# An AdaLN block with WKV attention and a mixture of experts: engine queues reordered from the third step on

## The chip, the cores and the metric

The kernel runs on one core of a Trainium2 chip. The metric is the device time of one execution in microseconds (us); the time of a kernel is the median of its runs. A difference of about 0.3% between two kernels can be told from none.

The engines are named as the profile names them: PE is TensorE (matmuls and transpositions), PEld its weight loads, DVE is VectorE, ACT is ScalarE, POOL is GpSimd, SP is SyncE, which here only issues transfers. Each engine works through its own queue of instructions in the order in which the program issues them, and waits where an instruction needs a semaphore.

## The reference

The input `x` is 4 x 1024 x 256 in float32. What is computed, cut to what matters:

```
mod = silu(c) @ wmod                          # six shift, scale and gate vectors per batch
h = layernorm(x) * (1 + ca) + sa
xk, xv, xr = mixes of h and h shifted by one token
k, v, r = xk @ Wk.T, xv @ Wv.T, xr @ Wr.T
wkv = the WKV scan over the 1024 tokens       # running maximum, running sums aa and bb
x = x + ga * ((sigmoid(r) * wkv) @ Wo.T)
h = layernorm(x) * (1 + cb) + sb
logits = h @ gate_w.T; top 2 of 8 experts, softmax over the two
y = sum over e of comb[e] * ((silu(h @ Wg[e]) * (h @ Wu[e])) @ Wd[e])
    + (silu(h @ sWg) * (h @ sWu)) @ sWd       # a shared expert of twice the width
x = x + gb * y
```

## The kernel before

**Tiling.** The 4096 tokens are cut into eight chunks of 512 (`NC` = 8, two per batch row). Most tiles hold the 256 features as two halves of 128 partitions with 512 tokens each; an operation on one half is 128x512, on both 128x1024. The eight experts of width 64 are taken in four pairs, and the shared expert makes a fifth block (`NB` = 5).

**Steps.** The work is pipelined over chunks. `step(n)` exists once for each engine and issues that engine's part for up to four chunks: the input norm, mixes and projections of chunk n + 1 (`nxt`), the end of attention and the second norm of chunk n (`cur`), the experts of chunk n - 1 (`prev`), and the last residual of chunk n - 2 (`before`). DVE also takes the input statistics of chunk n + 2 (`after`). The program runs a start for chunk 0, then step 0 (on ACT and DVE a `first_step` of its own), and steps 1 to 9. The order within a step is written out by hand in each engine's function, and this order with the semaphores decides when everything runs.

**Who does what in a step.**
- PE: `turn1` transposes the normalised input; `up(prev, i)`, i = 0 to 9, computes the experts' two products, six matmul groups on high and low parts each; `logits`, `turn_logits`, `turn_comb` and `spread_comb` belong to the routing; `attn` is the output projection of attention, `project(nxt, j)`, j = 0 to 5, are k, v and r in two halves each; `turn_attn` and `turn_down` transpose results back; `down(prev, 0)` and `down(prev, 1)` are the experts' second product; `turn2` transposes the second norm.
- ACT: `normalise1` and `normalise2` (4 instructions each), `affine1`, `affine2` (writes `h2_h` and `h2`), `part_mix`, `add_bias`, `tanh_r`, `silu`, the exponentials, `reciprocal_seed`, `attn_out`, `down_out`, and loads of function tables.
- DVE: `stats1`, `stats2`, `mix`, `scan_max`, `scan_sums`, `out_sums` 0 to 4, `divide` 0 to 3, `route` (19 small steps), `gate_up` (a product), `weigh`, `residual1`, `residual2`, and `low_part`, which subtracts `h2_h` from `h2` and releases `up(prev, 0)`.
- POOL: `rstd`, four small operations per norm and chunk, between the statistics on DVE and the normalisation on ACT.
- SP: loads of input chunks into two buffers `x_in`, stores of output chunks. A load into a buffer waits until `residual1` has read the chunk before it in that buffer.

The eight PSUM banks are shared: `mm` 0 to 3 by projections and `up`, `yo` 0 and 1 by `attn`, `turn_attn`, `down` and `turn_down`, `tp` and `cb` by the transpositions of norms and the routing. A wait ahead of each group on PE names whose reading frees its bank. The names in the profile's rows are those of the tiles: `n_xn` is a normalised chunk, `h_h` and `h_l` are `h2_h` and `h2_l`, `pool_x` holds `h2`, the weights `wmod` and two of the three `x1` buffers, `pool_n` holds `num` and `den`, `pool_g` the gates.

## Time and profile before

| | us |
|---|---|
| median of 3 runs | 409.92 |
| lowest, highest | 408.98, 410.11 |
| profiled execution, whole | 408.2 |
| its span | 406.3 |
| PE busy in the span | 366.6 |
| DVE busy | 334.6 |
| ACT busy | 295.2 |
| POOL busy | 44.7 |

The span is the time from the first to the last instruction that the profile shows; the whole time of the same execution is 1.9 us more. Busy times overlap, since engines work side by side. A timeline row gives the start, the time until the group's last end, and in brackets how long the engine was idle before and whose work ended that. Matmuls are pipelined, so the starts of two groups tell more than the length of one.

### The profile page before, as it was taken

The numbers are of one execution on the slowest core, as the hardware profiler recorded it, in microseconds if no ns is written. First come the engines' busy times: TensorE is split into PE (matmuls) and PEld (weight loads), VectorE is DVE, ScalarE is ACT, GpSimd is POOL, SyncE is SP. The second block draws the span as 40 slices with busy tenths as digits, with TensorE's granted clock in tenths as the row PEclk, the third lists the DMA queues.
The fourth block names the chain that finished last, engine by engine and source line by source line (L and its number), as shares of the span: only waits on it lengthen the run. The fifth ranks groups of instructions, "written<-read, shape, count | busy, mean of one in ns | idle before, by whom it ended". The sixth has DMA issues, their size and how long they took to land.

```text
span 406.3 us, 4276 instructions
## 1 busy us (share of the span) xinstructions
PE 366.6 (90%) x1348; PEld 224.8 (55%) x1348; DVE 334.6 (82%) x667; ACT 295.2 (73%) x466; POOL 44.7 (11%) x76
## 2 busy tenths in 40 slices
PE   4892873999999999999999999999999999969985
PEld 4561332756565845675476646574567455725752
DVE  4799989987989898999899898989898988541541
ACT  2699699846997589948994799759985894324332
POOL 4030013001400050002200230005000200010000
PEclk9995795799999999999999999999999999969999
DMA  8900010001000110011000300011001000100011
GB/s 287 268 5 1 0 52 0 0 2 52 0 2 0 52 52 2 0 52 54 0 2 2 103 0 0 2 53 50 2 1 52 2 0 0 52 2 0 0 53 52
DMA packets 15626, 13.27 MB, mean 33 GB/s; under 512 B 4690, under 2 KB 15092, under 8 KB 15604
## 3 DMA queue, kind: packets, MB, share of 16 engines
q1 hardware_dynamic: 15572, 12.99, 10.4%
q8 instruction: 11, 0.18, 0.2%
q14 instruction: 11, 0.09, 0.1%
q10 hardware_dynamic: 32, 0.01, 0.0%
HBM read 8.80 MB, written 4.19 MB: 32 GB/s over the span
## 4 chain that ended last, share of the span: by engine, by line
PE 63%; ACT 22%; DVE 9%; issue 3%; DMA 1%; SPq 0%; DVEq 0%; ACTq 0%
PE mm L737 29%; PE mm L632 10%; PE yo L765 7%; PE yo L650 7%; ACT arg L391 6%; ACT n_xn L326 5%; PE yo L659 3%; ACT arg L417 3%; ACT pool_x L366 2%; ACT h_h L365 2%; ACT kv L374 2%; DVE h_l L979 2%; ACT arg L405 1%; PE cb L749 1%; DVE mixed L879 1%
## 5 line engine op out<-in xcount | busy, mean ns | idle before, releaser
L632 PE MATMUL mm<-mixed,WT 128*128 128x512 f32 x192 | 87.5, 604 | 8.1 <-DVE mixed L879 8.1
L765 PE MATMUL yo<-act,w_dn 128*128 128x512 f32 x160 | 74.1, 613 | 5.4 <-DVE act L1056 5.4
L632 PEld LDWEIGHTS mm<-mixed,WT 128*128 128x128 f32 x192 | 36.3, 193 | 53.4 <-issue 39.6
L737 PE MATMUL mm<-h_h,w_up_h 128*128 128x512 f32 x160 | 55.2, 426 | 4.3 <-DVE h_l L979 4.3
L765 PEld LDWEIGHTS yo<-act,w_dn 128*128 128x128 f32 x160 | 30.8, 197 | 41.9 <-issue 35.6
L737 PE MATMUL mm<-h_l,w_up_h 128*128 128x512 f32 x160 | 51.1, 401 | 0.0
L737 PE MATMUL mm<-h_h,w_up_l 128*128 128x512 f32 x160 | 51.0, 400 | 0.0
L300 POOL TENSOR_TENSOR n_ve<-n_mv,small 128x4 f32<-128x4 f32 x16 | 8.2, 510 | 310.9 <-DVE n_mv L868 310.9
L374 ACT ACTIVATE kv<-mm,cols 128x512 f32<-128x512 f32 x32 | 21.8, 682 | 18.9 <-PE mm L632 18.9
L737 PEld LDWEIGHTS mm<-h_h,w_up_h 128*128 128x128 f32 x160 | 28.4, 192 | 12.6 <-DVE h_l L979 6.4
L737 PEld LDWEIGHTS mm<-h_h,w_up_l 128*128 128x128 f32 x160 | 30.6, 191 | 7.5
L737 PEld LDWEIGHTS mm<-h_l,w_up_h 128*128 128x128 f32 x160 | 30.6, 191 | 7.5
L879 DVE SCALAR_TENSOR_TENSOR mixed<-hT,cols,mixed 128x512 f32<-128x512 f32 x48 | 33.5, 742 | 0.3 <-ACT mixed L385 0.2
L438 ACT ACTIVATE pool_g<-mm 128x512 f32<-128x512 f32 x40 | 23.4, 586 | 10.4 <-PE mm L737 10.4
L385 ACT ACTIVATE mixed<-hT,rest 128x512 f32<-128x512 f32 x48 | 30.9, 710 | 0.0
L650 PE MATMUL yo<-pool_n,WT 128*128 128x512 f32 x64 | 28.8, 592 | 0.0
L1056 DVE TENSOR_TENSOR act<-cb,pool_g 128x512 f32<-128x512 f32 x24 | 16.5, 687 | 13.1 <-PE cb L749 13.1
L303 POOL TENSOR_TENSOR n_rstd<-n_ve,small 128x4 f32<-128x4 f32 x16 | 24.4, 1526 | 1.3
L1049 DVE TENSOR_TENSOR pool_g<-mm,pool_g 128x512 f32<-128x512 f32 x32 | 21.1, 680 | 3.7 <-PE mm L737 3.7
L979 DVE TENSOR_TENSOR h_l<-pool_x,h_h 128x1024 fp32r<-128x1024 f32 x8 | 9.8, 1225 | 17.3 <-ACT pool_x L366 17.3
L584 PE MATMUL tp<-ident,n_xn 128*128 128x128 f32 x88 | 15.2, 301 | 9.7 <-ACT n_xn L326 6.4
L468 ACT ACTIVATE combT<-cb 16x512 fp32r<-16x512 f32 x8 | 4.7, 588 | 26.2 <-PE cb L698 26.2
(149 smaller groups left out, 662.6 us busy)
## 6 DMA issues: line engine op xcount, KB each, us to landing
x_in<-in_L_attn_x_dram SPq DMA_DIRECT2D x8, 512.0 KB, 3.5
out_dram<-pool_x SPq DMA_DIRECT2D x5, 512.0 KB, 2.9
pool_x<-in_L_wmod_dram SPq DMA_DIRECT2D x2, 512.0 KB, 4.9
out_dram<-x_third SPq DMA_DIRECT2D x2, 512.0 KB, 2.9
pool_x<-in_L_wmod_dram SPq DMA_DIRECT2D x2, 256.0 KB, 4.0
pool_g<-in_L_ffn_Wg_dram SPq DMA_DIRECT2D x2, 256.0 KB, 5.0
pool_g<-in_L_ffn_Wu_dram SPq DMA_DIRECT2D x2, 256.0 KB, 4.4
w_dn<-in_L_ffn_Wd_dram SPq DMA_DIRECT2D x1, 512.0 KB, 3.9
```

Source lines behind the costliest of these rows:

```text
L303: nc.gpsimd.tensor_tensor(norm.rstd[:, :], norm.ve[:, :], small[:, 1, :], ALU.pow).then_inc(norm.pool_step, 1)
L326: nc.scalar.activation(norm.xn[:, t, :], src[:, t, :], ACT.Identity, bias=norm.shift[:, t:t + 1], scale=norm.rstd[:, t:t + 1]).then_inc(no ...
L374: nc.scalar.activation(kv[:, w, kc, :], mm[PROJECT_BANK[j]][:, :], ACT.Identity, bias=bias_cols[w][:, kc:kc + 1]).then_inc(kv_done, 1)
L385: nc.scalar.activation(mixed[:, w, kc, :], hT[c.half][:, kc, 0:CH], ACT.Identity, scale=rest[:, KH * w + kc:KH * w + kc + 1]).then_inc(par ...
L391: nc.scalar.activation(arg[:, j, h, :], tmp[:, h, :], ACT.Relu, scale=sign, bias=bias[:, h:h + 1]).then_inc(relu_done, 1)
L438: nc.scalar.activation(sg[:, e, :], mm[UP_BANK[2 * e]][:, :], ACT.Silu).then_inc(silu_done, 1)
L632: last = nc.tensor.matmul(mm[PROJECT_BANK[j]][:, :], WT[:, w, kc, oc * P:(oc + 1) * P], mixed[:, w, kc, :], start=(kc == 0), stop=(kc == K ...
L650: last = nc.tensor.matmul(yo[oc][:, :], WT[:, O, kc, oc * P:(oc + 1) * P], rw[:, kc, :], start=(kc == 0), stop=(kc == KH - 1))
L737: last = nc.tensor.matmul(mm[UP_BANK[i]][:, :], w[:, kc, gu, e * P:(e + 1) * P], rhs[:, kc, :], start=(n == 0), stop=(n == 3 * KH - 1))
L765: last = nc.tensor.matmul(yo[oc][:, :], w_dn[:, e, oc * P:(oc + 1) * P], act[:, e, :], start=(e == 0), stop=(e == NB - 1))
L879: nc.vector.scalar_tensor_tensor(out=mixed[:, w, kc, :], in0=hT[c.half][:, kc, 1:CH + 1], scalar=mix_cols[w][:, kc:kc + 1], in1=mixed[:, w ...
L1049: nc.vector.tensor_tensor(dst[:, e, :], mm[UP_BANK[2 * e + 1]][:, :], sg[:, e, :], ALU.mult).then_inc(prod_done, 1)
```

## The change

- **Queues.** What was `step` for all chunks is split into `first_step` (step 0), `second_step` (step 1) and `step` (from step 2, the third, on), each with its own order on PE, ACT and DVE.
- **Halves.** `attn`, `turn_attn`, `turn_down`, `turn2` and `tanh_r` are issued by half, each half with the semaphore count of its own half.
- **Routing.** `route` runs in four pieces on DVE, with products and mixes between them.
- **Statistics and sums.** In `step`, `stats2` and `stats1` stand together behind the last `weigh`, ahead of `scan_sums`; `out_sums` 2 and 4 and `low_part` go to the beginning of the following step; in `first_step` `scan_sums(nxt, 0)` stands between `stats2` and `stats1`.
- **First norm of chunk 0.** POOL computes only `rstd`; DVE subtracts the mean and multiplies in one instruction. K's transposition on PE stands behind those of the norm.
- **Output weights.** The copy of Wo, with its factor -0.5, goes from DVE to ACT.
- **Input buffers.** `x_in` has three buffers; a load waits for the chunk three before it.

```diff
-        x_in = [sb(f"x_in{h}", [P, TT, H]) for h in range(2)]
+        x_in = [sb(f"x_in{h}", [P, TT, H]) for h in range(3)]
...
-                wait(sp, x1_done, 2 * (c.n - 1))
-                sp.dma_start(x_in[c.half][:, :, :], x_chunks[c.n]).then_inc(x_loaded[c.half], 16)
+                wait(sp, x1_done, 2 * (c.n - 2))
+                sp.dma_start(x_in[c.n % 3][:, :, :], x_chunks[c.n]).then_inc(x_loaded[c.n % 3], 16)
...
+                direct = norm is norm1 and c.n == 0
...
+                if direct:
+                    return
...
+            ac.wait_ge(w_turned, O + 1)
+            nc.scalar.activation(WT[:, O, :, :], yo[1][:, :].rearrange("p (k h) -> p k h", k=KH), ACT.Identity,
+                                 scale=-0.5).then_inc(wo_done, 1)
...
             def turn2(c, kc):
                 pe.wait_ge(norm2.xn_done, TT * (c.n + 1))
                 if c.n:
-                    pe.wait_ge(act_done, NP * c.n)
+                    pe.wait_ge(act_done, NP * c.n - kc)
...
+            def attn(c, oc):
+                if oc == 0:
+                    pe.wait_ge(rw_done, c.n + 1)
...
                 elif c.n == 1:
-                    pe.wait_ge(x1_done, 2)
+                    pe.wait_ge(x1_done, oc + 1)
                 else:
-                    pe.wait_ge(yT_done, KH * (c.n - 1))
+                    pe.wait_ge(yT_done, KH * (c.n - 2) + oc + 1)
...
+            def turn_attn(c, k):
                 pe.wait_ge(oT_done, KH * (c.n + 1))
                 if c.n >= 2:
-                    pe.wait_ge(x2_done, 2 * (c.n - 1))
-                turn_out(oT, attn_turned)
+                    pe.wait_ge(x2_done, 2 * (c.n - 2) + k + 1)
+                turn_out(oT, k, attn_turned)
...
+            def turn_down(c, k):
                 pe.wait_ge(yT_done, KH * (c.n + 1))
                 if chunk(c.n + 2):
-                    pe.wait_ge(oT_done, KH * (c.n + 3))
-                turn_out(yT, down_turned)
+                    pe.wait_ge(oT_done, KH * (c.n + 2) + k + 1)
+                turn_out(yT, k, down_turned)
...
             def first_step():
...
                 stats2(cur)
+                scan_sums(nxt, 0)
                 stats1(after)
-                scan_sums(nxt, 0)
                 scan_sums(nxt, 1)
...
-            turn_square(K, mm[2])
             pe.wait_ge(norm1.xn_done, TT)
             turn(norm1, chunk(0), 0, tp)
             turn(norm1, chunk(0), 1, cb)
+            turn_square(K, mm[2])
```

The new `step`, from the third step on, on PE, on ACT and on DVE:

```
turn1(nxt, 0); up(prev, 0); logits(prev); turn1(nxt, 1); up(prev, 1); up(prev, 2); turn_logits(prev)
up(prev, 3); up(prev, 4); attn(cur, 0); project(nxt, (0,)); attn(cur, 1); project(nxt, (1,))
turn_down(before, 0); up(prev, 5); turn_down(before, 1); turn_comb(prev); turn_attn(cur, 0)
up(prev, 6); spread_comb(prev, 1); up(prev, 7); spread_comb(prev, 2); up(prev, 8); up(prev, 9)
spread_comb(prev, 3); spread_comb(prev, 4); turn_attn(cur, 1); project(nxt, (2, 3, 4))
down(prev, 0); turn2(cur, 0); turn2(cur, 1); project(nxt, (5,)); down(prev, 1)
```

```
affine2(prev, 0); affine2(prev, 1); normalise1(nxt); reciprocal_seed(cur); affine1(nxt, 0); SILU table
tanh_r(cur, 0); affine1(nxt, 1); logits_out(prev); tanh_r(cur, 1); silu(prev, 0); down_out(before, 0)
part_mix(nxt, 0); part_mix(nxt, 1); silu(prev, 1); part_mix(nxt, 2); down_out(before, 1)
add_bias(nxt, 0); gap_out(prev); attn_out(cur, 0); silu(prev, 2); attn_out(cur, 1); add_bias(nxt, 1)
comb_out(prev); silu(prev, 3); state_falls(nxt, 0); silu(prev, 4); EXP table
state_exponentials(nxt, 0); state_falls(nxt, 1); add_bias(nxt, 2); output_falls(nxt)
state_exponentials(nxt, 1); add_bias(nxt, 3); normalise2(cur); output_exponential(nxt, 2 and 3)
```

```
low_part(prev); out_sums(cur, 2); out_sums(cur, 4); divide(cur, 0 to 3); gate_up(prev, 0)
route(prev, 0 to 3); mix(nxt, 0); route(prev, 4 to 8); gate_up(prev, 1); route(prev, 9 to 11)
mix(nxt, 1); route(prev, 12 to 18); scan_max(nxt, 0); residual2(before, 0); mix(nxt, 2)
residual2(before, 1); gate_up(prev, 2); weigh(prev, 1); scan_max(nxt, 1); weigh(prev, 2)
gate_up(prev, 3); residual1(cur, 0); gate_up(prev, 4); weigh(prev, 3); residual1(cur, 1)
weigh(prev, 4); stats2(cur); stats1(after); scan_sums(nxt, 0 and 1); out_sums(nxt, 0, 3, 1)
```

**ACT at the border of two steps.** Before, from the last output falls of one step to the seed of the reciprocal of the next:

```order
L391 ACTIVATE arg<-tmp,minus_tf 128x512 x2
L326 ACTIVATE n_xn<-x_third,n_shift,n_rstd 128x256 x4
L417 ACTIVATE arg<-arg 128x1024 x2
L326 ACTIVATE n_xn<-x_in,n_shift,n_rstd 128x256 x4
L365 ACTIVATE h_h<-tp,modc 128x512
L366 ACTIVATE pool_x<-tp,modc 128x512
L365 ACTIVATE h_h<-cb,modc 128x512
L366 ACTIVATE pool_x<-cb,modc 128x512
L423 ACTIVATE arg<-pool_n 128x1024
L425 ACTIVATE arg<-arg 128x1024
```

After, the same place:

```order
L396 ACTIVATE arg<-tmp,minus_tf 128x512 x2
L410 ACTIVATE arg<-arg 128x512 x2
L379 ACTIVATE kv<-mm,cols 128x512
L331 ACTIVATE n_xn<-x_third,n_shift,n_rstd 128x256 x4
L422 ACTIVATE arg<-arg 128x1024 x2
L370 ACTIVATE h_h<-tp,modc 128x512
L371 ACTIVATE pool_x<-tp,modc 128x512
L370 ACTIVATE h_h<-cb,modc 128x512
L371 ACTIVATE pool_x<-cb,modc 128x512
L331 ACTIVATE n_xn<-x_in,n_shift,n_rstd 128x256 x4
L428 ACTIVATE arg<-pool_n 128x1024
L430 ACTIVATE arg<-arg 128x1024
```

The four `affine2` instructions (`h_h`, `pool_x`) stand ahead of `normalise1` (`n_xn<-x_in`), and the exponentials of the second half with their bias behind the output falls.

**PE at the end of a step.** Before, from the last two `spread_comb` to `turn1` of the next step (`mm<-mixed,WT` are projections, `yo<-act,w_dn` is `down`, the transpositions of `n_xn` are `turn2` and then `turn1`):

```order
L749 MATMUL cb<-combT,sel 128x512
L749 MATMUL tp<-combT,sel 128x512
L632 MATMUL mm<-mixed,WT 128x512 x8
L765 MATMUL yo<-act,w_dn 128x512 x5
L584 MATMUL tp<-ident,n_xn 128x128 x4
L584 MATMUL cb<-ident,n_xn 128x128 x4
L765 MATMUL yo<-act,w_dn 128x512 x5
L584 MATMUL tp<-ident,n_xn 128x128 x4
```

After, the same place:

```order
L795 MATMUL cb<-combT,sel 128x512
L795 MATMUL tp<-combT,sel 128x512
L707 MATMUL yo<-ident,oT 128x128 x4
L679 MATMUL mm<-mixed,WT 128x512 x6
L811 MATMUL yo<-act,w_dn 128x512 x5
L631 MATMUL tp<-ident,n_xn 128x128 x4
L631 MATMUL cb<-ident,n_xn 128x128 x4
L679 MATMUL mm<-mixed,WT 128x512 x2
L811 MATMUL yo<-act,w_dn 128x512 x5
L631 MATMUL tp<-ident,n_xn 128x128 x4
```

A half of `turn_attn` came in, and the last projection went from the place ahead of the first `down` to behind `turn2`.

**DVE, weighs and statistics.** Before, from behind the second `weigh` to the end of `stats1` (`act` is written by the third and fourth `weigh`):

```order
L965 TENSOR_TENSOR x_third<-yo,x_in 128x512 x2
L864 BN_STATS n_stats<-x_third 128x6 x4
L866 MEMSET pace 128x1
L868 BN_AGGR n_mv<-n_stats 128x2 x4
L879 SCALAR_TENSOR_TENSOR mixed<-hT,cols,mixed 128x512 x2
L1049 TENSOR_TENSOR pool_g<-mm,pool_g 128x512
L1056 TENSOR_TENSOR act<-cb,pool_g 128x512
L1056 TENSOR_TENSOR act<-tp,pool_g 128x512
L864 BN_STATS n_stats<-x_in 128x6 x4
L866 MEMSET pace 128x1
L868 BN_AGGR n_mv<-n_stats 128x2 x4
```

After, the same place:

```order
L1146 TENSOR_TENSOR pool_g<-mm,pool_g 128x512
L1062 TENSOR_TENSOR x_third<-yo,x_in 128x512
L1146 TENSOR_TENSOR pool_g<-mm,pool_g 128x512
L1153 TENSOR_TENSOR act<-cb,pool_g 128x512
L1062 TENSOR_TENSOR x_third<-yo,x_in 128x512
L1153 TENSOR_TENSOR act<-tp,pool_g 128x512
L959 BN_STATS n_stats<-x_third 128x6 x4
L961 MEMSET pace 128x1
L963 BN_AGGR n_mv<-n_stats 128x2 x4
L959 BN_STATS n_stats<-x_in 128x6 x4
L961 MEMSET pace 128x1
L963 BN_AGGR n_mv<-n_stats 128x2 x4
```

The mix (`mixed`) is gone to an earlier place, the two residuals (`x_third<-yo,x_in`) stand apart, and both statistics follow the last `weigh` (`act<-tp`).

## Rows read from the trace of the kernel before

**Rows 1.** The page: span, then busy time, share of the span, instructions.
```profile
span 406.3 us, 4276 instructions
...
PE 366.6 (90%) x1348; PEld 224.8 (55%) x1348; DVE 334.6 (82%) x667; ACT 295.2 (73%) x466; POOL 44.7 (11%) x76
```

**Rows 2.** Windows: length, busy per engine (count), PE clock, DMA share, GB/s.
```profile
42.00:70.70 28.70, 19.55 (x52) 9.60 (x52) 26.14 (x45) 25.59 (x41) 4.88 (x8) 0.80 0.06 18
...
203.14:246.80 43.66, 43.08 (x160) 26.10 (x160) 40.49 (x79) 35.53 (x57) 5.68 (x8) 1.00 0.08 25
...
333.12:372.60 39.48, 34.72 (x129) 21.64 (x129) 22.07 (x50) 16.58 (x26) 1.60 (x4) 0.91 0.04 14
```

**Rows 3.** Timeline, PE: start, length, operation, idle before and its releaser.
```profile
236.16 4.45 PE L765 MATMUL yo<-act,w_dn 128*128 128x512 f32 x10
240.45 0.60 PE L584 MATMUL tp<-ident,n_xn 128*128 128x128 f32 x4
...
245.62 0.60 PE L584 MATMUL tp<-ident,n_xn 128*128 128x128 f32 x4
246.80 0.73 PE L737 MATMUL mm<-h_h,w_up_h 128*128 128x512 f32 x2 [0.58 <-DVE h_l L979]
```

**Rows 4.** Timeline, ACT, the end of the same step.
```profile
231.03 0.69 ACT L374 ACTIVATE kv<-mm,cols 128x512 f32<-128x512 f32 x1 [1.62 <-PE mm L632]
...
236.91 2.06 ACT L326 ACTIVATE n_xn<-pool_x,n_shift,n_rstd 128x256 f32<-128x256 f32 x4
...
240.77 2.06 ACT L326 ACTIVATE n_xn<-x_in,n_shift,n_rstd 128x256 f32<-128x256 f32 x4
...
244.72 0.77 ACT L366 ACTIVATE pool_x<-cb,modc 128x512 f32<-128x512 f32 x1
```

**Rows 5.** Timeline, DVE, the same stretch.
```profile
233.69 0.68 DVE L1056 TENSOR_TENSOR act<-tp,pool_g 128x512 f32<-128x512 f32 x1
...
243.22 1.23 DVE L930 TENSOR_TENSOR pool_n<-pool_n,arg 128x1024 f32<-128x1024 f32 x1
245.53 1.22 DVE L979 TENSOR_TENSOR h_l<-pool_x,h_h 128x1024 fp32r<-128x1024 f32 x1 [1.08 <-ACT pool_x L366]
```

**Rows 6.** Timeline, DVE, at the start.
```profile
8.10 1.38 DVE L1145 TENSOR_SCALAR n_xn<-x_in,n_rstd,n_shift 128x256 f32<-128x256 f32 x4 [1.98 <-POOL n_shift L309]
...
37.33 0.68 DVE L1162 TENSOR_SCALAR WT<-yo 128x512 f32<-128x512 f32 x1
```

**Rows 7.** Timeline, DVE, the first step.
```profile
59.18 1.41 DVE L864 BATCH_NORM_STATS2 n_stats<-x_in 128x6 f32<-128x256 f32 x4 [1.69 <-DMA x_in<-in_L_attn_x_dram]
...
69.43 1.22 DVE L979 TENSOR_TENSOR h_l<-pool_x,h_h 128x1024 fp32r<-128x1024 f32 x1
```

**Rows 8.** Timeline, ACT and POOL, the first step.
```profile
64.67 2.07 ACT L326 ACTIVATE n_xn<-x_in,n_shift,n_rstd 128x256 f32<-128x256 f32 x4
...
57.85 1.01 POOL L303 TENSOR_TENSOR n_rstd<-n_ve,small 128x4 f32<-128x4 f32 x1
...
61.72 1.86 POOL L303 TENSOR_TENSOR n_rstd<-n_ve,small 128x4 f32<-128x4 f32 x1
```

**Rows 9.** Timeline, PE, first step and the last two.
```profile
70.71 1.22 PE L737 MATMUL mm<-h_h,w_up_h 128*128 128x512 f32 x2 [1.41 <-DVE h_l L979]
...
346.01 1.06 PE L659 MATMUL yo<-ident,yT 128*128 128x128 f32 x8 [0.96 <-ACT oT L445]
...
360.13 7.32 PE L765 MATMUL yo<-act,w_dn 128*128 128x512 f32 x10 [3.80 <-DVE act L1056]
...
391.93 8.85 PE L765 MATMUL yo<-act,w_dn 128*128 128x512 f32 x20 [1.58 <-DVE act L1056]
```

**Rows 10.** Timeline, DVE and ACT, the step of the last chunk.
```profile
356.49 1.41 DVE L864 BATCH_NORM_STATS2 n_stats<-pool_x 128x6 f32<-128x256 f32 x4
...
359.40 0.68 DVE L1056 TENSOR_TENSOR act<-tp,pool_g 128x512 f32<-128x512 f32 x1
...
360.26 2.07 ACT L326 ACTIVATE n_xn<-pool_x,n_shift,n_rstd 128x256 f32<-128x256 f32 x4 [4.98 <-POOL n_shift L309]
```

More of the change, by code:

```diff
@@ L296, in rstd @@
             def rstd(norm, c):
+                direct = norm is norm1 and c.n == 0
+                step = 3 * c.n - (2 if norm is norm1 and c.n else 0)
                 wait(pool, norm.mv_done, TT * (c.n + 1))
@@ L503, in first_step, with second_step @@
                 output_exponential(nxt, 3)
-            def step(n):
-                before, prev, cur, nxt = (chunk(n + d) for d in (-2, -1, 0, 1))
-                normalise1(nxt)
+            def second_step():
+                prev, cur, nxt = (chunk(n) for n in range(3))
                 affine2(prev, 0)
                 affine2(prev, 1)
+                normalise1(nxt)
                 reciprocal_seed(cur)
@@ L574, in _ @@
             first_step()
-            for n in range(1, NC + 2):
+            second_step()
+            for n in range(2, NC + 2):
                 step(n)
@@ L769, in turn_down, with first_step, second_step @@
             @of_chunk
[L770 removed]
+            def turn_down(c, k):
                 pe.wait_ge(yT_done, KH * (c.n + 1))
                 if chunk(c.n + 2):
[L773 to L777 removed]
+                    pe.wait_ge(oT_done, KH * (c.n + 2) + k + 1)
+                turn_out(yT, k, down_turned)
+            def first_step():
+                cur, nxt = chunk(0), chunk(1)
                 turn1(nxt, 0)
+                turn1(nxt, 1)
+                project(nxt, (0, 1))
+                attn(cur, 0)
+                attn(cur, 1)
+                turn_attn(cur, 0)
+                turn_attn(cur, 1)
+                project(nxt, (2, 3, 4, 5))
+                turn2(cur, 0)
+                turn2(cur, 1)
+            def second_step():
+                prev, cur, nxt = (chunk(n) for n in range(3))
                 up(prev, 0)
+                turn1(nxt, 0)
                 up(prev, 1)
[L781 removed]
                 logits(prev)
                 up(prev, 2)
+                turn1(nxt, 1)
                 up(prev, 3)
@@ L806, in step @@
                 down(prev, 0)
-                turn2(cur)
+                turn2(cur, 0)
+                turn2(cur, 1)
+                down(prev, 1)
+            def step(n):
+                before, prev, cur, nxt = (chunk(n + d) for d in (-2, -1, 0, 1))
+                turn1(nxt, 0)
+                up(prev, 0)
+                logits(prev)
+                turn1(nxt, 1)
+                up(prev, 1)
+                up(prev, 2)
+                turn_logits(prev)
+                up(prev, 3)
+                up(prev, 4)
+                attn(cur, 0)
+                project(nxt, (0,))
+                attn(cur, 1)
+                project(nxt, (1,))
+                turn_down(before, 0)
+                up(prev, 5)
+                turn_down(before, 1)
+                turn_comb(prev)
+                turn_attn(cur, 0)
+                up(prev, 6)
+                spread_comb(prev, 1)
+                up(prev, 7)
+                spread_comb(prev, 2)
+                up(prev, 8)
+                up(prev, 9)
+                spread_comb(prev, 3)
+                spread_comb(prev, 4)
+                turn_attn(cur, 1)
+                project(nxt, (2, 3, 4))
+                down(prev, 0)
+                turn2(cur, 0)
+                turn2(cur, 1)
+                project(nxt, (5,))
                 down(prev, 1)
@@ L1093, in first_step, with second_step @@
                 out_sums(nxt, 4)
-            def step(n):
-                before, prev, cur, nxt, after = (chunk(n + d) for d in (-2, -1, 0, 1, 2))
-                divide(cur, 0)
-                divide(cur, 1)
-                divide(cur, 2)
-                divide(cur, 3)
+            def second_step():
+                prev, cur, nxt, after = (chunk(n) for n in range(4))
+                for n in range(4):
+                    divide(cur, n)
                 mix(nxt, 0)
```

204 lines of the change are left out of this document (133 added, 71 removed).

## Prediction

> **What bounds the kernel now.** I read the page first: in a span of 406.3 us PE is busy for 366.6 and DVE for 334.6 [rows 1]. The windows by stage say where the other 40 us of PE lie. In an ordinary step, 203.14 to 246.80, PE works 43.08 of 43.66 us; the stretch from 42.00 to 70.70 has only 19.55 of 28.70, at a granted clock of 0.80; the step of the last chunk, 333.12 to 372.60, has 34.72 of 39.48, at 0.91 [rows 2]. So there are three kinds of loss: a small gap in each ordinary step, a filling stretch, an emptying stretch. No matmul is added or removed, so what the change can give lies in these gaps and in matmuls at the lower clock.
>
> In the ordinary step the gap is the 0.58 us before the first `up` matmul at 246.80, released by DVE's `h_l` (`low_part`) [rows 3]. DVE ran `h_l` at 245.53 after waiting 1.08 us for ACT's last `pool_x` [rows 5], and ACT wrote that in `affine2`, 244.72 to 245.49, behind `normalise1`, 240.77 to 242.83 [rows 4]. This is the chain to shorten.
>
> **The start.** The direct first norm drops two POOL operations of 0.20 us on the way to `rstd`, and `turn(norm1, 0)` now stands before the transposition of K. DVE waited 1.98 us for `n_shift` and normalised at 8.10 [rows 6]; that would now be about 7.55. PE was then still in its modulation matmuls, so the real profit is K's place: ACT's first `hT` comes 0.9 us earlier, but DVE's `square(V)` still waits for the same transposition, and `mix(0,0)` starts only 0.3 us earlier. Behind it DVE is never idle until its constants at 37.33, where `square(O)`, 0.68 us, goes to ACT [rows 6]; of it 0.5 is gained, since one wait behind it was covered. On ACT it costs about as much, but ACT has over 1 us to spare there. Start: **0.8**.
>
> **First step.** DVE waited 1.69 us for chunk 2's load, to 59.18 [rows 7]. The third buffer lets that load go early, and `scan_sums(1,0)` fills the place as well. On ACT `normalise1(2)`, 64.67 to 66.74, now stands behind `affine2(0)` [rows 8], so `affine2` starts 1.97 us earlier, and 0.8 for the start. `low_part(0)` at 69.43 [rows 7] then starts at the later of DVE's 69.43 - 0.8 - 1.69 = 66.9 and ACT's 69.4 - 0.8 - 1.97 = 66.6: about 66.9. `up(0,0)` moves from 70.71 [rows 9] to 68.2: **2.5**, the start's 0.8 included.
>
> POOL costs a little of it. Its `n_rstd` took 1.01 us at 57.85, with DVE idle, and 1.86 at 61.72, with DVE in `scan_sums` [rows 8]. `scan_sums(1,0)` now stands right behind `stats2(0)`, so the slower one falls on norm 2. The four operations began 0.3 before 57.85, and at the ratio 1.86 to 1.01 their 1.9 us become 3.5: 57.55 - 0.8 + 3.5 = 60.3 against ACT's free time at 60.0, a loss of **0.3** if it isn't hidden. The Trainium skill has the rule (SBUF — State Buffer, section SBUF: two separate sides): a DVE instruction with two SBUF inputs and a GpSimd instruction that reads SBUF exclude each other. By that rule, which speaks against this place, the sum is 0.3 smaller than by the row with DVE idle; the trace agrees with it.
>
> **Second step.** Its PE work is the same. Relative to `up(0,0)` ACT is 2 us later now, since `normalise1(2)` follows `affine2`: I replay its queue with the trace's durations and find `lgT` ready 9.6 us after `up(0,0)`, where PE wants it at 9.3. Price **0.3**. At this step's end `out_sums 3` stands ahead of `low_part(1)` on DVE. One such operation is 1.14 us, and `out_sums 1` ended at 244.4 in the same place of a later step, so `low_part` would start at 245.6 instead of 245.53 [rows 5]: this first boundary gains nothing, though ACT has the data 2 us earlier.
>
> **Ordinary steps, from the third.** PE's queue has the same work with as many changes between transpositions and matmuls, so its floor is 43.08 us. A projection (four passes of 0.43 us, from ten in 4.29 between 236.16 and 240.45 [rows 3]) moves behind `turn2`, so that `down(.,0)` and `turn2` come 1.7 us sooner. I replayed one step for three engines from `up(prev,0)` at 0; margins between what is ready and what PE wants:
> - `rw` ready 7.1, `attn(.,0)` wants it at 8.8; `mix(nxt,0)` 9.8 against 10.5.
> - last `weigh` 27.5 against `down(.,0)` at 30.8. It ended at 234.37 before [rows 5]; being ahead of both statistics now it isn't the problem.
> - `stats2` ends at 29.2, 1.1 later than now; POOL needs 1.9 to 3.5, ACT is free at 32.3 because the falls of half 1 fill its idle 1.62 us before 231.03 [rows 4]; `normalise2` ends at about 34.5 (before: 238.97 in the trace, that is 35.8 [rows 4]), `turn2` wants it at 35.1. Margin 0.6, the thinnest.
> - `affine2` then ends at 39.1, `out_sums 1` at 40.5, `low_part` at 41.7; PE wants it at 43. `normalise1` is ready at 41, `turn1` wants it at 42.6.
>
> All are kept, so the 0.58 us gap closes at four boundaries, 203.14 and 246.80 [rows 2] and one on either side of them (the one at 333 has no gap): 4 x 0.58 = **2.3**. Nothing is given for the finer routing or the halves of `attn` here: the routing ended before PE wanted it, and PE's own time for `turn_comb` stays.
>
> **The last chunk.** PE stood 3.80 us before `down(6,0)` at 360.13, for DVE's `act`, the last `weigh` at 359.40 [rows 9, 10]; its ten matmuls then took 7.32 us against 4.45 for ten at 236.16 [rows 9, 3], so 2.9 to 3.0 were at the lower clock; `turn2(7)` came at 367.29. Three edits work here. `turn_down(.,0)` needs one half of `oT`, which removes the 0.96 us at 346.01 [rows 9]; the second half of `turn_attn` leaves the way of the `up` matmuls (0.4); and the weighs stand before `stats2` (1.41 us and its aggregates [rows 10]). In the replay the last `weigh` ends near 356.4 instead of 360.1, and `down(6,0)` starts after some 1.9 us of idle PE. Does the clock fall? After 3.80 us it did, after the 1.58 us at 391.93 it didn't: twenty matmuls took 8.85 [rows 9]. 1.9 is much nearer the second; I take no fall. Then `down` ends at 360.8, and `turn2(7)` waits for `normalise2(7)`. That isn't earlier than now: PE and DVE arrive 1.8 us sooner, but a product and three weighs or residuals stand before `stats2` that stood after. It ends at 360.26 + 2.07 = 362.3 [rows 10]. `turn2` moves from 367.3 to 362.4: **4.9**. If the clock falls all the same, `down` takes 7.2 from 356.5 and the gain is 3.6. Behind `turn2` `down(6,1)` hides `affine2` and `low_part` as now, and the last step keeps its queue in effect: 0.
>
> **Sum.** 2.5 - 0.3 (POOL) - 0.3 (second step) + 2.3 + 4.9 = 9.1 us. The profiled execution took 408.2 us, with 406.3 of span; it would come to 399.1, span 397.2. It lies 1.7 below the median of the three runs, 409.92; from that median the same sum gives 400.8.
>
> **Rivals.**
> - *A new wait in the ordinary steps.* The 0.6 us margin before `turn2` is a sum of some twenty durations. If it turns into a wait of 0.3 to 1.2 us in each of five steps, 1.5 to 6.0 us are lost: 402.3 to 406.8, say 403.8. For it: the wait would stand where PE is 1.7 us earlier. Against it: ACT works 35.53 of 43.66 us in a step [rows 2]. Chance 0.2.
> - *The clock falls in the last chunk's `down`*, the rest as forecast: 402.1. Chance 0.13.
> - *More than I count*: the first boundary closes too, or `stats2(7)` comes 1 to 2 us sooner, 398.5. Chance 0.07.
> - *Slower.* `turn1(nxt,0)` heads PE's queue in each step, ahead of `up`. `normalise1`, its source, ended at 242.83 with 2.8 us to spare [rows 4, 3]; it now stands behind the four `affine2` instructions, 2.66 us. If ACT doesn't get earlier elsewhere (its falls still waiting for `scan_max(nxt,1)`, which now stands behind two products and a weigh), 0.1 is left, and each further us of ACT is a us of idle PE in six steps. It outweighs the 9.1 from 1.5 us a step on (9.1 / 6); at 2 us the time is 400.8 + 12 = 412.8. Against it: in the replay `scan_max(nxt,1)` ends at 22.7, when ACT reaches those falls at 26.4. Chance 0.05.
> - *The order does nothing net*: ends gained, steps lost, 409 to 411. Chance 0.02.
>
> **Numbers.** Forecast 400.8, chance 0.53, its own range 399.3 to 402. The range of eight in ten goes from the case of more gain to most of the new waits: 398 to 405. A difference of 0.3%, 1.2 us, is what a measurement of this kernel can tell: faster 0.93, same 0.02, slower 0.05.
>
> **What the changed profile would show.** `up` of the third step on with no gap before it, steps of 43.1 us between first `up` matmuls; `up(0,0)` at about 68.2; `square(O)` on ACT; no wait of DVE for a load near 59; ten `down` matmuls in 4.4 us at the last chunk with an idle PE of about 1.9 before and 1.5 behind them. Wrong would be: PE waiting for `n_xn` before `turn2` or `turn1` in the middle of the kernel, or 7 us for those ten matmuls.

## The result and the profile after

The changed kernel takes 398.02 us in the median of four runs (397.29 to 399.27), against 409.47 in four runs of the kernel before (408.98 to 410.11): 11.4 us less, a ratio of 0.9723 with a 95% interval of 0.9693 to 0.9753. The forecast was 400.8, range 398 to 405. The median lies at the lower end of that range, and below the 399.3 to 402 in which the forecast itself was given its chance of 0.53. The profiled execution took 397.29 us, its span is 395.5. Against the span before, 406.3 [rows 1], that is 10.8 us, where the sum had 9.1.

The page of the kernel after, its counterpart to [rows 1], and the granted clock in 40 slices:

```profile
span 395.5 us, 4302 instructions
...
PE 361.1 (91%) x1348; PEld 222.8 (56%) x1348; DVE 332.5 (84%) x666; ACT 295.2 (75%) x467; POOL 52.2 (13%) x74
...
PEclk9995795899999999999999999999999999999999
```

PE has as many instructions as before and is busy 5.5 us less: 2.75 in the last chunk's step (31.97 for 34.72 [rows 2]), where the matmuls at the lower clock are gone (no slice below 9 behind the eighth), and 0.41 in each ordinary step (42.67 for 43.08), where a group's tail is now covered by the group that follows. POOL's busy time has grown by 7.5 us with two operations fewer.

The windows after, counterparts to [rows 2]: from the first projection of chunk 1 to the first `up`, an ordinary step, and the step of the last chunk.

```profile
40.91:67.77 26.86, 18.58 (x48) 8.96 (x48) 25.96 (x45) 24.64 (x40) 6.71 (x8) 0.82 0.06 20
...
199.09:241.76 42.67, 42.67 (x164) 26.09 (x162) 40.14 (x79) 35.22 (x57) 7.05 (x8) 1.00 0.08 25
...
326.33:361.25 34.92, 31.97 (x131) 20.70 (x129) 20.56 (x48) 16.47 (x25) 1.61 (x4) 1.00 0.05 15
```

The ordinary step has no idle time of PE, in 42.67 us where it was 43.66; the last chunk's step runs at a clock of 1.00 where it had 0.91.

The timeline of PE after, around the end of an ordinary step (counterpart to [rows 3]):

```profile
225.07 5.32 PE L679 MATMUL mm<-mixed,WT 128*128 128x512 f32 x12
230.22 4.46 PE L811 MATMUL yo<-act,w_dn 128*128 128x512 f32 x10
234.52 0.60 PE L631 MATMUL tp<-ident,n_xn 128*128 128x128 f32 x4
234.95 0.60 PE L631 MATMUL cb<-ident,n_xn 128*128 128x128 f32 x4
235.39 1.88 PE L679 MATMUL mm<-mixed,WT 128*128 128x512 f32 x4
237.11 4.46 PE L811 MATMUL yo<-act,w_dn 128*128 128x512 f32 x10
241.40 0.60 PE L631 MATMUL tp<-ident,n_xn 128*128 128x128 f32 x4
241.76 0.71 PE L783 MATMUL mm<-h_h,w_up_h 128*128 128x512 f32 x2
```

The timelines of ACT and of DVE in the same step (to [rows 4] and [rows 5]):

```profile
231.80 2.06 ACT L331 ACTIVATE n_xn<-pool_x,n_shift,n_rstd 128x256 f32<-128x256 f32 x4
...
237.64 0.78 ACT L371 ACTIVATE pool_x<-cb,modc 128x512 f32<-128x512 f32 x1
238.31 2.07 ACT L331 ACTIVATE n_xn<-x_in,n_shift,n_rstd 128x256 f32<-128x256 f32 x4
```

```profile
239.58 1.21 DVE L1076 TENSOR_TENSOR h_l<-pool_x,h_h 128x1024 fp32r<-128x1024 f32 x1
```

`turn1`, at 241.40, has its source `n_xn` at 240.38 (238.31 + 2.07), and `up`, at 241.76, has `h_l` at 240.79 (239.58 + 1.21): both with 1.0 us to spare. Before, `h_l` ended at 246.75, 1.13 us behind the start of `turn1` [rows 3, 5].

Step by step, how much earlier each point of PE's queue comes, in the two profiled executions:

| point on PE | before | after | gain so far | forecast so far |
|---|---|---|---|---|
| first projection of chunk 1 | 42.03 | 40.94 | 1.09 | 0.8 |
| `up(0,0)` | 70.71 | 67.78 | 2.93 | 2.2 |
| first `up` of the third step | 115.76 | 113.74 | 2.02 | 1.9 |
| first `up` four steps on | 290.47 | 284.42 | 6.05 | 4.2 |
| first `up` of the last chunk's step | 332.55 | 326.33 | 6.22 | 4.2 |
| first `up` of the last step | 372.06 | 361.25 | 10.81 | 9.1 |
| last `down` | 391.93 | 381.11 | 10.82 | 9.1 |

### The profile page after: what moved, and what is told of

It reads as the page before. It is cut to its first block, busy times and chain, and to the rows that moved or that the text cites. A ratio compares the mean times of both kernels' runs of the same rounds, so it can differ in the third digit from the quotient of the medians.

```text
span 395.5 us, 4302 instructions
## 1 busy us (share of the span) xinstructions
PE 361.1 (91%) x1348; PEld 222.8 (56%) x1348; DVE 332.5 (84%) x666; ACT 295.2 (75%) x467; POOL 52.2 (13%) x74
## 4 chain that ended last, share of the span: by engine, by line
PE 79%; DVE 12%; ACT 3%; issue 3%; DMA 1%; POOL 0%; SPq 0%; DVEq 0%; POOLq 0%
PE mm L783 29%; PE mm L679 17%; PE yo L811 15%; PE yo L698 6%; PE yo L707 3%; PE tp L631 3%; DVE mixed L974 2%; DVE n_stats L959 1%; PE cb L795 1%; DVE state L990 1%; ACT n_xn L331 1%; DMA pool_x<-in_L_wmod_dram 1%; DVE state L1009 1%; PE yo L908 1%; PE cb L744 1%
## 5 line engine op out<-in xcount | busy, mean ns | idle before, releaser
L679 PE MATMUL mm<-mixed,WT 128*128 128x512 f32 x192 | 88.4, 603 | 7.1 <-DVE mixed L974 7.1
L811 PE MATMUL yo<-act,w_dn 128*128 128x512 f32 x160 | 71.3, 593 | 3.3 <-DVE act L1153 3.3
L303 POOL TENSOR_TENSOR n_ve<-n_mv,small 128x4 f32<-128x4 f32 x16 | 9.3, 581 | 297.6 <-DVE n_mv L963 297.6
L783 PEld LDWEIGHTS mm<-h_h,w_up_h 128*128 128x128 f32 x160 | 27.6, 191 | 11.3 <-DVE h_l L1076 4.8
L698 PE MATMUL yo<-pool_n,WT 128*128 128x512 f32 x64 | 29.6, 592 | 0.0
L631 PEld LDWEIGHTS tp<-ident,n_xn 128*128 128x128 f32 x88 | 11.9, 155 | 17.7 <-ACT n_xn L331 11.9
L990 DVE TENSOR_TENSOR_SCAN state<-decay,state,kv 128x512 f32<-128x512 f32 x16 | 20.5, 1281 | 0.8 <-ACT kv L379 0.6
```

The costliest lines, as they stand in the source:

```text
L631: last = nc.tensor.transpose(dst[:, t * P:(t + 1) * P], norm.xn[:, t, kc * P:(kc + 1) * P], ident[:, :])
L679: last = nc.tensor.matmul(mm[PROJECT_BANK[j]][:, :], WT[:, w, kc, oc * P:(oc + 1) * P], mixed[:, w, kc, :], start=(kc == 0), stop=(kc == K ...
L698: last = nc.tensor.matmul(yo[oc][:, :], WT[:, O, kc, oc * P:(oc + 1) * P], rw[:, kc, :], start=(kc == 0), stop=(kc == KH - 1))
L783: last = nc.tensor.matmul(mm[UP_BANK[i]][:, :], w[:, kc, gu, e * P:(e + 1) * P], rhs[:, kc, :], start=(n == 0), stop=(n == 3 * KH - 1))
L811: last = nc.tensor.matmul(yo[oc][:, :], w_dn[:, e, oc * P:(oc + 1) * P], act[:, e, :], start=(e == 0), stop=(e == NB - 1))
L990: nc.vector.tensor_tensor_scan(state[:, 0, h, 1:CH + 1], decay[:, h:h + 1].to_broadcast([P, CH]), kv[:, K, h, :], state[:, 0, h, 0:1], ALU ...
```

## The experiments

Eleven kernels. Each was timed beside the kernel before on the same chip, with its own ratio; medians of the kernel before were 410.22 (28 runs), 408.41 (7) and 410.20 (7) in the three groups. What happens before the first logits scatters by some 3 us from one execution to the next (last section) and shifts all that follows, so sizes of some tenths are read in the profiles. The kernels made from the one before are read from the logits of chunk 0 on. Those made from the one after are read from the logits of chunk 1 on, because their second step scatters too: it took 41.93 to 42.50 us in five kernels whose order there is the same, with waits of PE for `sgm` of 0.21 to 0.79 us. A period is the time from one chunk's logits to the next; it was 43.67 in the kernel before and is 42.67 after.

**affine2 first, alone** (on the kernel before, from the second step on).

```diff
-                normalise1(nxt)
                 affine2(prev, 0)
                 affine2(prev, 1)
+                normalise1(nxt)
```

> The kernel before, with only affine2(prev) put ahead of normalise1(nxt) on ACT from the second step on. Theory A (the chain of the prediction: normalise1, affine2, low_part, up): the two gaps before up close, and counted from start to start a gap is 0.83 us (1.18 from turn1 to up before, 0.35 after), so five of them give 4.2 us, ratio about 0.990, with normalise1 ready 0.2 us before turn1 wants it. Rival B (ACT as a whole is late, and the order only moves the wait): PE now waits for normalise1 at turn1 instead of for low_part at up, and the gain is under 1.5 us, ratio 0.996 to 1.000.

Measured: 407.70, ratio 0.9951 (0.9925 to 0.9976), some 2 us faster, of which the profiles show 1.07 (298.00 us from the logits of chunk 0 to those of chunk 7, against 299.07). That is rival B's size, not the 4.2 us of theory A: the periods are 43.31 to 43.67. Its timelines of PE and of ACT:

```profile
245.44 0.66 PE L584 MATMUL tp<-ident,n_xn 128*128 128x128 f32 x4
245.85 0.71 PE L737 MATMUL mm<-h_h,w_up_h 128*128 128x512 f32 x2
```

```profile
240.65 0.78 ACT L365 ACTIVATE h_h<-tp,modc 128x512 fp32r<-128x512 f32 x1 [0.22 <-PE tp L584]
...
243.31 2.07 ACT L326 ACTIVATE n_xn<-x_in,n_shift,n_rstd 128x256 f32<-128x256 f32 x4
```

The 0.58 gap before `up` is gone, and from `down` to `up` it is 0.51 less (4.97 against 5.48). But `turn1` now starts when `normalise1` ends (243.31 + 2.07 = 245.38), 4.56 us behind the start of `down`, whose ten matmuls need 4.29, and `affine2` itself waits for `turn2`. So ACT, not the order of two of its groups, was late by more than the gap showed: swapping them hands a part of the wait from `up` to `turn1`. The rest of the gain is lost again some 4 us further on, where PE waits before `up(prev, 2)` for `sgm`, which ACT writes in `tanh_r`: 0.15 us in one step, and in the next 0.38, with another 0.10 before `attn`, all read from the starts. To win, ACT has to come earlier or `turn2` has to.

**Three moves together, on the kernel before**, from the second step on: affine2 first as above, the falls on ACT, and the last projection on PE.

```diff
-                add_bias(nxt, 2)
                 state_falls(nxt, 1)
+                add_bias(nxt, 2)
...
-                project(nxt, (2, 3, 4, 5))
+                project(nxt, (2, 3, 4, 5) if n == 0 else (2, 3, 4))
                 down(prev, 0)
                 turn2(cur)
+                if n:
+                    project(nxt, (5,))
```

> The kernel before with the three orders done from the second step on: affine2 ahead of normalise1, the falls of half 1 ahead of add_bias 2, projection 5 behind turn2. With affine2 alone 1.3 us were gained, and affine2 then waited 0.22 us for turn2. Theory A (the three together suffice): the 0.83 us of each of five borders close, 3.5 to 4.2 us less than before, ratio 0.990, steps of 42.8. Rival B (DVE's place of low_part behind out_sums, or of mix 2, also needs changing): at most 2 us less, with PE waiting for DVE at down, which now stands 1.7 us earlier against weigh 4 at 234.4.

Measured: 403.77, ratio 0.9858 (0.9799 to 0.9917). Periods 42.91, no idle PE from the second step to the last chunk. These three moves are 0.76 of the 1.00 us per step. The other 0.24 belongs to the rest of the new order, which was not taken apart; the starts of PE's matmuls show where it sits. The projections wait 0.17 for the last mix, as in the kernel before (see the ordinary steps in the next section), and the first `down` loses 0.08 at the last `weigh`, which ends at 232.59 where `down` starts at 232.67. Of the 4.83 us that the profile shows from the logits of chunk 0 to those of chunk 7, 1.05 are the last chunk's, where the ten matmuls took 6.25 us instead of 7.32 behind the same idle time.

**The same three undone in the kernel after**, the falls there with the exponentials and the bias in the old order too:

```diff
-                state_falls(nxt, 1)
                 add_bias(nxt, 2)
-                output_falls(nxt)
+                state_falls(nxt, 1)
                 state_exponentials(nxt, 1)
                 add_bias(nxt, 3)
+                output_falls(nxt)
```

> The changed kernel with three orders undone from the third step on: normalise1 ahead of affine2, the falls of half 1 behind add_bias 2 (and the output falls behind add_bias 3), and projection 5 ahead of down. Theory A (these three together closed the gap): ACT reaches affine2 at 153.5, low_part ends at 157.3 and up starts 0.9 to 1.0 us later than 156.42 in each of the steps; period 43.6, 4 to 5 us more in all, ratio to before about 0.984. Rival B (DVE's order, with weighs, mixes and sums placed anew, closed it): 0 to 1 us more.

Measured: 403.23, ratio 0.9850 (0.9786 to 0.9914). Periods 43.70, as long as before, and the wait is back at the same place, larger. PE's timeline:

```profile
200.79 0.60 PE L631 MATMUL tp<-ident,n_xn 128*128 128x128 f32 x4
202.16 0.73 PE L783 MATMUL mm<-h_h,w_up_h 128*128 128x512 f32 x2 [0.77 <-DVE h_l L1075]
```

The two experiments agree from both sides: the three moves give 0.76 us per step without the rest, and the rest gives an ordinary step nothing without them.

**Each of the three undone alone, in the kernel after.** First the order of `affine2`:

```diff
+                normalise1(nxt)
                 affine2(prev, 0)
                 affine2(prev, 1)
-                normalise1(nxt)
```

> The changed kernel with, from the third step on, normalise1 back ahead of affine2 on ACT. Theory A (the gap closed because ACT as a whole is earlier and turn2 comes sooner; the order of these two is redundant): affine2 ends at 154.95 in the step before 156.42, low_part at 156.2, up wants it at 156.42; nothing is lost, steps stay at 42.7 us. Rival B (this order closes the gap, as the prediction said): the gap comes back, steps of 43.5 us, 3 to 4 us more in all.

Measured: 401.14, ratio 0.9802 (0.9730 to 0.9874), periods 43.28, that is 0.61 more per step, between what the two theories had. A third party has a part in it: POOL. The timelines of POOL and ACT in this kernel:

```profile
146.46 1.18 POOL L303 TENSOR_TENSOR n_ve<-n_mv,small 128x4 f32<-128x4 f32 x1
147.71 1.90 POOL L306 TENSOR_TENSOR n_rstd<-n_ve,small 128x4 f32<-128x4 f32 x1
149.69 0.89 POOL L311 TENSOR_TENSOR n_mr<-n_mv,n_rstd 128x4 f32<-128x4 f32 x1
150.66 1.10 POOL L314 TENSOR_TENSOR n_shift<-small,n_mr 128x4 f32<-128x4 f32 x1
```

```profile
151.79 2.08 ACT L331 ACTIVATE n_xn<-x_in,n_shift,n_rstd 128x256 f32<-128x256 f32 x4 [0.53 <-POOL n_shift L314]
```

Both statistics now stand together on DVE, so POOL's second set of four runs under `scan_sums` and takes 5.3 us, and `normalise1` waits 0.53 us for it; the four `affine2` instructions behind it, and `up`, come later by that. `affine2` first is what hides this: in the kernel after the second set ends (at 236.26) while ACT is in `affine2` (235.66 to 238.42).

Then the falls alone, with the edit shown above, and the projection alone:

```diff
-                project(nxt, (2, 3, 4))
+                project(nxt, (2, 3, 4, 5))
...
-                project(nxt, (5,))
```

> The changed kernel with ACT's old order of falls, exponentials and bias at the end of each later step (the falls of half 1 behind add_bias 2, the output falls last), affine2 still first and projection 5 still behind turn2. Theory A (each of the three moves carries part of the 1.00 us per step): ACT then waits about 1.2 us for the projection before add_bias 2, normalise2 comes about 1.2 us later, turn2 or the gap behind it takes some 0.5 us of it; periods near 43.2 us instead of 42.67, in five steps 2.6 us more, ratio to the kernel before about 0.979. Theory B (affine2 first is enough, the falls are cover only): periods 42.7, no change, ratio 0.972.

> The changed kernel with all projections ahead of down(prev,0), as before, the rest unchanged. down and turn2 stand 1.7 us later in PE's queue, so turn1 and up of the next step follow turn2 by 1.7 us less. Theory A (the place of projection 5 is needed): affine2 ends near 153.8 instead of 153.0 in the step shown, low_part waits for it and turn1 to up has a gap of 0.2 to 0.4 us again; periods about 43.0, in five steps 1.5 us more, ratio about 0.976. Theory B (with affine2 first there is enough time without it): periods 42.7, no change; 0.972.

Measured: 401.79 (0.9794, 0.9741 to 0.9846) and 401.59 (0.9784, 0.9742 to 0.9826). From the logits of chunk 1 to those of chunk 7 it is 247.82 us in the kernel after, 250.44 without the new falls, 250.14 with the projections together: 2.62 and 2.32 more, where 2.6 and 1.5 were expected. PE's timelines, of the first and of the second, and a weight load of the second a few us into a step:

```profile
237.87 0.66 PE L631 MATMUL tp<-ident,n_xn 128*128 128x128 f32 x4 [0.30 <-ACT n_xn L331]
```

```profile
196.63 4.46 PE L811 MATMUL yo<-act,w_dn 128*128 128x512 f32 x10
201.19 0.65 PE L631 MATMUL tp<-ident,n_xn 128*128 128x128 f32 x4
```

```profile
162.76 0.30 PEld L783 LDWEIGHTS mm<-h_h,w_up_h 128*128 128x128 f32 x2 [0.38 <-ACT sgm L435]
```

With the old falls `turn2` waits 0.30 us for `normalise2`. With the projections together `turn1` starts 4.56 us behind `down` instead of 4.29 and `up` 0.41 behind it instead of 0.36: it is `turn1` that waits for `normalise1`, not `up` for `h_l` as expected. That is 0.32 per step; the periods are 42.98 to 43.38, so 0.31 to 0.71 longer. What goes beyond 0.32 stands a little further on, where PE meets a late ACT again: by the starts of the step of the last row, 0.19 us before `turn1(nxt, 1)`, and 0.21 before `up(prev, 2)`, for `sgm` (the 0.38 in the row is the idle time of the weight loads, which run ahead of the matmuls). By the same measure `normalise1` first costs 2.45, and all three undone cost 4.16. Each move alone is worth 2.3 to 2.6 us, and none is a spare: with any one missing more than half of the loss of all three is back, so their worths do not add up.

**The third input buffer**, added alone to the kernel before, and taken away alone from the kernel after:

```diff
-        x_in = [sb(f"x_in{h}", [P, TT, H]) for h in range(2)]
+        x_in = [sb(f"x_in{h}", [P, TT, H]) for h in range(3)]
```

The load's wait changes with it, as in the kernel after.

> The kernel before, with only the third input buffer. Theory A: in the first step low_part starts at the later of DVE and ACT, ACT's affine2 ends at 69.4 as before, so removing DVE's wait of 1.69 us for the load gives nothing: 0 to 0.1 us, ratio 1.000. Rival B: DVE's chain of sums sets the first step, and 1.5 to 1.7 us are gained, ratio 0.996.

> The changed kernel with two input buffers. Theory A (the buffer is the cover of the new order): each load waits for residual1 of the chunk two before, which now ends 2.3 us ahead of stats1, and lands some 3.5 us after; DVE waits 1.4 to 1.8 us in each of five ordinary steps, of which its slack of about 1.0 before up hides a part: 2.5 to 4 us more, ratio 1.006 to 1.010. Rival B (DVE's slack and later places hide all): no change, ratio 1.000 within 0.002. In the first step neither expects a wait, since scan_sums stands between the load and stats1.

Measured: 410.57, ratio 1.0013 (0.9992 to 1.0034), alone: nothing. The wait of 1.69 us for the load is gone from the first step, and from `turn2` to `up(0,0)` it is even 0.40 longer (8.18 against 7.78): `stats1` now follows `stats2` at once, POOL's second set runs under the scans and takes 5.3 us here too, and `normalise1` waits for it. ACT's timeline:

```profile
67.14 2.08 ACT L326 ACTIVATE n_xn<-x_in,n_shift,n_rstd 128x256 f32<-128x256 f32 x4 [0.28 <-POOL n_shift L309]
```

Taken away from the kernel after: 401.07, ratio 0.9797 (0.9760 to 0.9835), 2.0 us more between the logits of chunk 1 and 7, less than the 2.5 to 4 expected. DVE's timeline without it:

```profile
145.76 1.41 DVE L959 BATCH_NORM_STATS2 n_stats<-x_in 128x6 f32<-128x256 f32 x4 [1.17 <-DMA x_in<-in_L_attn_x_dram]
```

The buffer matters only because `stats1` now follows `stats2` directly: with two buffers its load, which waits for `residual1`, has not landed, and `scan_sums`, `out_sums` and `low_part` queue behind. In the first step of the new order the buffer gives nothing: from `turn2` to `up(0,0)` it is 5.82 us with two buffers and with three. There `scan_sums(1,0)` ahead of `stats1` covers the load already.

**The last chunk: weighs ahead of `stats2`, alone on the kernel before; and `stats2` ahead of the last weigh in the kernel after.**

```diff
-                stats2(cur)
+                if nxt:
+                    stats2(cur)
...
                 weigh(prev, 4)
+                if not nxt:
+                    stats2(cur)
```

> The kernel before, with stats2 of the last chunk alone put behind the last weigh. down of chunk 6 then starts at about 358.4 after 2.2 us of idle PE instead of 3.8. Theory A (the clock does not fall after 2.2 us): ten matmuls in 4.4 us, normalise2 comes 1.8 us later and turn2 at 364.2 instead of 367.3: 3.1 us less, ratio 0.992. Rival B (it falls): ten matmuls in 7.2 us, turn2 at 365.6: 1.7 us less, ratio 0.996, and a granted clock under 1 in that stretch.

> The changed kernel with stats2 of the last chunk ahead of the last weigh, all else unchanged. PE should then stand about 3.5 us (1.75 and the 1.7 us of the statistics) before down(6,0). Theory A (the granted clock falls behind an idle time of that length): the ten matmuls take 6.2 to 7.3 us instead of 4.56, the idle time before turn2(7) falls to nothing, and the logits of chunk 7 come 2.5 to 3 us later, ratio about 0.979. Theory B (the clock holds): ten matmuls in 4.5 us, the statistics' 1.7 us come out of the 1.20 us idle before turn2(7), 0 to 0.6 us in all, ratio 0.973.

Measured: 406.60, ratio 0.9933 (0.9901 to 0.9965); and 402.23, ratio 0.9799 (0.9753 to 0.9844). The groups of ten `down` matmuls of PE's timelines: in the kernel after (with the row behind it), in the kernel before with the weighs moved, in the kernel after with the statistics ahead of the last weigh, and in the kernel before with the three moves.

```profile
350.66 4.56 PE L811 MATMUL yo<-act,w_dn 128*128 128x512 f32 x10 [1.75 <-DVE act L1153]
356.42 0.66 PE L631 MATMUL tp<-ident,n_xn 128*128 128x128 f32 x4 [1.20 <-ACT n_xn L331]
```

```profile
361.08 6.26 PE L765 MATMUL yo<-act,w_dn 128*128 128x512 f32 x10 [1.91 <-DVE act L1056]
```

```profile
354.85 7.47 PE L811 MATMUL yo<-act,w_dn 128*128 128x512 f32 x10 [3.65 <-DVE act L1153]
```

```profile
356.91 6.25 PE L765 MATMUL yo<-act,w_dn 128*128 128x512 f32 x10 [3.80 <-DVE act L1058]
```

After 1.75 us of idle time the ten matmuls took 4.56, in the kernel after and likewise in the six variants of it that leave this place alone. After 1.91 they took 6.26; after 3.65 and 3.80, between 6.25 and 7.47 (the kernel before: [rows 9]). In the kernel after, the statistics ahead of the last weigh cost 3.39 us, a little more than theory A's 2.5 to 3 (logits of chunk 7 to those before: 38.30 against 34.91): 1.90 more idle time, and 1.54 more from the start of `down` to `turn2` (7.30 against 5.76), since 1.20 of the slower matmuls' time had been idle anyway. On the kernel before the move gives 2.95 (36.53 against 39.48), 1.89 of it idle time and 1.06 from the start of `down` to `turn2` (6.09 against 7.15). That is nearly theory A's 3.1, but not by its mechanism: the matmuls did slow down, as rival B had it, only fewer of them.

**The second step repaired.** PE waits 0.79 us there for `sgm`, written by `tanh_r`, which stands behind `affine1(nxt, 0)` on ACT. In this kernel the SILU table and both `tanh_r` go ahead of it, and the falls take the later steps' order.

```diff
-                affine1(nxt, 0)
                 nc.scalar.preload_act_table_set(SILU_SET)
                 tanh_r(cur, 0)
                 tanh_r(cur, 1)
+                affine1(nxt, 0)
...
-                add_bias(nxt, 2)
                 state_falls(nxt, 1)
+                add_bias(nxt, 2)
```

> The changed kernel with two changes in ACT's second step alone: the table load and tanh_r ahead of affine1(nxt, 0), and the falls of half 1 and the output falls ordered as in the later steps. Theory A (in the second step PE's wait of 0.79 us before up 2 is ACT's tanh being late behind affine1, and the wait for normalise1 at its end is ACT being late): 0.8 to 1.4 us less than the changed kernel, the second step 45.0 instead of 46.0 us. Rival B (the tanh's place only moves the wait to lgT and the mixes): 0 to 0.3 us less.

Measured: 398.36, ratio 0.9719 (0.9656 to 0.9782). The profile shows the wait gone and the second step 1.05 us shorter than in the profile of the kernel after (41.45 against 42.50), 1.06 in all up to the last `down`; against the other executions of the same second step it is 0.48 to 0.95 shorter, as their wait for `sgm` was smaller. The new order of the falls showed nothing there: `turn1` still starts 4.56 us behind `down` at the step's end. A median of four runs, with starts that scatter by more than that, can't tell it from the kernel after: here the eight projection passes at 41.5 took 6.71 us where they took 5.21.

## Why the prediction was right, point by point

- **Start, 0.8: right in size, its causes not shown.** 1.09 in these executions. Of it 0.30 is the first weights' landing (PE's first matmul on `wmod` at 5.87 against 6.17). From there to the first projection is 0.31 less, for which the forecast gave K's transposition 0.3, and from there to that of chunk 1 0.48, for which it gave Wo's copy on ACT 0.5. No experiment took these or the direct norm apart. The first projection alone starts anywhere from 15.27 to 15.92 in executions of one and the same start, so the 0.31 is not clear of the scatter; the 0.48 is (26.07 us, against 25.59 or 25.60 in all six profiles of the new start in which the first 24 passes took 10.57).
- **First step, 2.5 less 0.3: 2.93**, of which the start is 1.09. POOL's `n_rstd` did fall under DVE's scan and took 1.86 us, as the row said, and the Trainium skill's rule (SBUF — State Buffer, section SBUF: two separate sides, an exclusive lock of the pair that DVE and GpSimd share) again agrees with the trace; but it isn't paid, since `n_shift` ended at 59.73 and ACT was free only at 59.84. The 0.3 was a term that cover had already cancelled, by 0.1 us. From `turn2` to `up(0,0)` it is 5.82 instead of 7.78. The buffer had no part in that: DVE's wait is gone without it, by the filling with `scan_sums`, and the buffer alone in the old order, with ACT's queue as it was, shortened nothing. DVE and ACT arrive together now (`affine2` ends at 66.47, `low_part` starts at 66.50), so both halves of the edit were needed, as the prediction had it; ACT's half alone was not run.
- **Second step, 0.3: 0.9, three times the price.** The replay saw that PE would wait for `lgT` (it did, 0.17) and missed `sgm`, 0.79, one place ahead of it in PE's queue; the repair above takes that wait away. How long it is varies, though, 0.21 to 0.79 over the executions, and 0.79 is the worst of them. That this step's end gains nothing was nearly right: `turn1` waits 0.27 for `normalise1` and `up` follows it after 0.69 for `h_l` (112.46 + 1.22), 0.24 less in all than before (5.24 against 5.48 from `down` to `up`).
- **Ordinary steps, 2.3: 4.03 in four, 4.20 with the fifth; in size the term most off.** The mechanism and the number of boundaries were right, the size was not. The step that failed is "so its floor is 43.08 us" and with it "4 x 0.58": a busy time counts the pipeline's tail of the last group before a wait. From the start of `turn1` to the start of `up` it was 1.18 us [rows 3] and is 0.36, so the wait cost 0.82, not 0.58. Another 0.17 sat where no idle time is printed: sixteen projection passes took 7.04 us from start to start (229.12 to 236.16) and take 6.87 (5.15 for twelve, 1.72 for four), because the last mix is ready earlier: before, it ended at 232.57, and the ninth and tenth pass started at 232.62 and 233.16, 0.50 and 0.54 behind the pass ahead instead of 0.43. The sum, 0.99, is the measured step.
- **The margin of 0.6 us before `turn2`: 0.66.** `normalise2` ends at 233.86 and `turn2` starts at 234.52. That it was thin is what the kernel with the old falls shows, 0.30 us late. The rival "a new wait" needed just this. "Slower" needed ACT late at `turn1`: there 1.0 us was to spare where the replay had 1.6, and before `up` 1.0 where it had 1.3. The replay was a little kind to ACT, but not by enough to matter.
- **Last chunk, 4.9: 4.59.** Idle 1.75 for a forecast 1.9, clock kept, `turn2` at 356.42. The missing 0.3 is `stats2(7)`, which starts 24.20 us behind the step's first `up` where it was 23.94; the forecast had it no later than before. The rival with a falling clock was nearer than it looked: at 1.91 us of idle time, in another kernel, the matmuls did slow down, and the forecast of no fall rested on 1.58 and 3.80 alone.
- **Last step, 0: 0.01.**
- **The sum.** From 9.1 to 10.8: 1.9 more in the ordinary steps, 0.3 at the start, 0.4 in the first step; 0.6 less in the second step and 0.3 less in the last chunk. The sum owes a part of its closeness to such opposite errors. The two medians are 11.4 apart; the 0.6 beyond 10.8 is less than the single executions scatter. The measured 398.0 is nearest to the rival "more than I count" (398.5, chance 0.07), but not for its reasons: the first boundary gave 0.24 us, and `stats2(7)` came later, not sooner.

## What to carry to other kernels

When PE waits for the end of a chain, measure the loss from the start of the group ahead to the start of the group that waited, and compare groups that show no idle time by their starts too: busy time hid 0.4 us of 1.0 per step here. A wait of 0.6 us may stand for an engine that is late by more: moving one group shortened a step by 0.36 us at most, three moves on two engines together by 0.76, with no idle time left. Undone one at a time, each of the three cost more than half of what all three cost, so a move can't be priced by taking it out alone. A buffer that buys nothing alone can be the condition for an order that does, so test it in both kernels.
